# TensorE multiplies the identity with itself in its waits, in a four-stage layer kernel

## The reference

```
m = mean(group); s = var(group)          # over all 128*128 points and the 2 channels
norm(v) = (v - m) / sqrt(s + eps)
x = x + L0(norm(x))   # layer norm, then attention along the rows: 4 heads of 32, softmax, gate, output product
x = x + L1(norm(x))   # windowed attention (8 windows, top 4) folded with a 3x3 depthwise convolution
x = x + L2(norm(x))   # per row of 4 x 32: top 9 of a correlation, an ODE of 8 Runge-Kutta steps as a polynomial
x = x + L3(norm(x))   # products of x and its transpose, of row, column and diagonal sums; relu
```

## Time and profile before

| | |
|---|---|
| time, median of 3 runs (lowest to highest) | 1100.49 us (1098.49 to 1101.67) |
| time of the profiled execution | 1099.39 us |
| its span, first to last instruction | 1097.3 us |
| TensorE busy | 1027.7 us, 94% of the span |
| TensorE weight loads | 731.4 us, 67% |
| VectorE | 762.3 us, 69% |
| ScalarE | 510.6 us, 47% |
| GpSimd | 409.7 us, 37% |
| mean granted clock of TensorE | 0.967 |

### The profile page before, as it was taken

How to read it: one execution, slowest core, us unless ns; L and a number is a source line. 1 busy time by engine, 2 the same in 40 slices (tenths; PEclk the granted TensorE clock), 3 DMA queues, 4 the chain that set the end, 5 groups by cost and what they waited for, 6 DMA issues and landing times. The chain is left out here.

```text
span 1097.3 us, 24506 instructions
## 1 busy us (share of the span) xinstructions
PE 1027.7 (94%) x8864; PEld 731.4 (67%) x8864; DVE 762.3 (69%) x3657; ACT 510.6 (47%) x1101; POOL 409.7 (37%) x555
## 2 busy tenths in 40 slices
PE   5897999999999699779999999999999999999978
PEld 3434888888887343356777777777777777677743
DVE  2686999999998423456767676767776676767445
ACT  2475776776776201133433434343443434343346
POOL 0054666766666200011323333232323233332328
PEclk9899999999999699959999999999999999999979
DMA  8000000000000000000000000000000000000025
GB/s 177 2 0 2 3 2 3 2 3 3 2 3 2 1 1 1 10 1 2 1 1 1 1 1 1 1 1 1 1 1 1 1 1 1 1 1 1 1 56 174
DMA packets 14044, 12.99 MB, mean 12 GB/s; under 512 B 3300, under 2 KB 11748, under 8 KB 13924
## 3 DMA queue, kind: packets, MB, share of 16 engines
q1 hardware_dynamic: 12548, 10.84, 4.0%
q10 hardware_dynamic: 1376, 0.59, 0.3%
HBM read 5.14 MB, written 4.19 MB: 9 GB/s over the span
## 5 line engine op out<-in xcount | busy, mean ns | idle before, releaser
L1615 PE MATMUL quad<-theta,nat 128*128 128x512 f32 x512 | 240.8, 593 | 0.0
L738 POOL TENSOR_TENSOR nat<-nat,arena 128x512 f32<-128x512 f32 x128 | 131.4, 1048 | 48.2 <-DVE arena L793 48.2
L1623 PEld LDWEIGHTS quad<-flat 128*128 128x128 f32 x768 | 104.3, 190 | 46.9 <-ACT flat L1409 24.1
L1615 PEld LDWEIGHTS quad<-theta,nat 128*128 128x128 f32 x512 | 87.5, 191 | 61.7 <-issue 61.7
L1623 PE MATMUL quad<-flat 128*128 128x128 f32 x768 | 124.6, 285 | 2.1 <-ACT flat L1409 1.0
L793 DVE CUSTOM_DVE_ANT_0 nat<-quad,arena 128x128 f32<-128x128 f32 x512 | 112.7, 286 | 6.4 <-PE quad L881 6.4
L1409 ACT ACTIVATE flat<-quad 128x256 f32<-128x256 f32 x192 | 73.4, 383 | 74.5 <-PE quad L1623 58.0
L755 ACT ACTIVATE nat<-pair 128x512 f32<-128x512 f32 x128 | 69.5, 596 | 66.5 <-PE pair L889 66.5
L1366 POOL COPY img<-flat 64x256 f32<-64x256 f32 x63 | 25.0, 398 | 186.2 <-DVE nat L1524 171.7
L760 ACT ACTIVATE nat<-nat 128x512 f32<-128x512 f32 x128 | 77.0, 630 | 4.0 <-POOL nat L738 4.0
L1531 DVE MAX8 arena<-nat 128x8 f32<-128x128 f32 x128 | 28.0, 281 | 71.3 <-ACT nat L1445 71.3
(11 more groups left out here) (386 smaller groups left out, 2300.7 us busy)
## 6 DMA issues: line engine op xcount, KB each, us to landing
out<-nat SPq DMA_DIRECT2D x16, 256.0 KB, 2.0
flat<-img SPq DMA_DIRECT2D x2, 640.0 KB, 8.6
flat<-img SPq DMA_DIRECT2D x1, 512.0 KB, 4.9
const<-in_constants ACTq DMA_DIRECT2D x1, 400.5 KB, 3.1
flat<-img SPq DMA_DIRECT2D x1, 256.0 KB, 3.1
arena<-in_L_conv_Ws SPq DMA_DIRECT2D x1, 240.0 KB
nat<-in_x SPq DMA_DIRECT2D x4, 0.2 KB, 12.1
arena<-in_L_conv_Wq ACTq DMA_DIRECT2D x1, 32.0 KB, 6.5
```

The lines of the kernel that those rows point to most:

```text
L738: pool.tensor_tensor(scored, scored, of_head(least[b], h).broadcast_to([128, ROWS, L]), ALU.subtract).then_inc(lowered, 1)
L1615: return pe.matmul(m.quad[:, n, :], vT[:, col(n)], m.theta[:, part, :], start=(part == 0), stop=False, skip_group_check=True)
L1623: last = pe.matmul(m.quad[:, row, place * C:(place + 2) * C], a8[g % 2][:, col(row)], zs[half][k % 2][:, n, :], start=False, stop=(k == 2) ...
```

## The change

A new helper `keep_clock(pe, bank, times)` issues `times` products of the 128 x 128 identity with itself into the first 128 columns of a bank. Nobody reads them, and they carry no semaphore. They are put at these places of TensorE's list:

- at the end of `load_and_prepare`: 6
- in every norm: 2 (layers 0 and 2) or 4 (layers 1 and 3) ahead of the first product's wait, 2 between the two products, 3 behind the second
- in the attention's last step (the one that has no `past` group): 4 ahead of the wait for the copy, 5 ahead of the wait for the output's factor; 6 at the end of the block
- at the end of `layer1`: 13
- in `layer2`, step 0: 6 ahead of `turn_xs(0)`, 13 ahead of the wait for the diagonal, 9 at the end of the step; 11 at the end of the block

Apart from that the two products with the shift column in `layer1` now load this column 128 times (a broadcast operand), and so write all 128 rows of the banks 4 and 5 in place of row 64 alone. The row that is read is the same.

```diff
+    def keep_clock(self, pe, bank, times):
+
+        ident = self.k("ident", 128)
+        for _ in range(times):
+            pe.matmul(bank[:, 0:128], ident, ident, start=True, stop=True)
@@ load_and_prepare, tensor
             turn_banks(at_bank, BANKS)
+            m.keep_clock(pe, m.bank[4], 6)
@@ group_norm, tensor
+            m.keep_clock(pe, m.bank[7], 2 if layer % 2 == 0 else 4)
             pe.wait_ge(S("mean"), layer + 1)
             pe.matmul(acc[0:rows, 0:1], alike, mv[:, 0:1], start=True, stop=True).then_inc(S("group_mean"), 1)
+            m.keep_clock(pe, m.bank[7], 2)
             pe.wait_ge(S("var"), layer + 1)
             pe.matmul(acc[0:rows, 1:2], alike, e, start=True, stop=True).then_inc(S("group_var"), 1)
+            m.keep_clock(pe, m.bank[7], 3)
@@ layer0_attention, tensor, in the loop
                 if older:
+                    if not past:
+                        m.keep_clock(pe, m.bank[7], 4)
                     pe.wait_ge(rwide_ready, g - 1)
...
                 if older:
+                    if not past:
+                        m.keep_clock(pe, m.bank[7], 5)
                     pe.wait_ge(gated_ready, g - 1)
@@ behind the loop
+            m.keep_clock(pe, m.bank[7], 6)
@@ layer1, tensor
-            pe.matmul(B[4][C:C + 1, :], fold[:, 128:129], m.taps1[:, 0:512], start=True, stop=True)
-            pe.matmul(B[5][C:C + 1, 0:C], fold[:, 128:129], m.taps1[:, 512:TAPS * C], start=True, stop=True).then_inc(S("row_made"), 1)
+            fold_row = fold[:, 128:129].broadcast_to([C + 1, 128])
+            pe.matmul(B[4][:, :], fold_row, m.taps1[:, 0:512], start=True, stop=True)
+            pe.matmul(B[5][:, 0:C], fold_row, m.taps1[:, 512:TAPS * C], start=True, stop=True).then_inc(S("row_made"), 1)
@@ behind its loop
                 close(i)
+            m.keep_clock(pe, B[7], 13)
@@ layer2, tensor, in the loop
                 if s == 0:
+                    m.keep_clock(pe, B[1], 6)
                     turn_xs(0)
...
+                if s == 0:
+                    m.keep_clock(pe, B[1], 13)
                 if p is not None:
                     pe.wait_ge(diag_added, p + 1)
...
                     if c == LAST:
                         horner(c, 1, 2)
+                if s == 0:
+                    m.keep_clock(pe, B[1], 9)
+            m.keep_clock(pe, m.quad[:, 0, :], 11)
```

## The result

| | before | changed |
|---|---|---|
| median | 1101.08 us (1098.49 to 1103.51, 4 runs) | 1091.69 us (1091.51 to 1094.11, 4 runs) |
| ratio | | 0.992, 95% interval 0.9895 to 0.9944 |
| profiled execution, span | 1099.39, 1097.3 us | 1094.11, 1092.3 us |
| mean granted clock | 0.967 | 0.972 |

The change, 105 added products in all, makes the kernel faster by 9.4 us, 0.8%. A second measurement of the same source (e11_changed_again) gave 1092.08 us and a ratio of 0.9918 (0.9897 to 0.9939). The forecast was 1089.0.

The account below looks back on a forecast made before the run. TensorE bounds the loops; at the seams engines wait and its clock halves. Layers 0 to 3 gain 2.0 + 2.0 + 3.3 + 3.8 = 11.1, less 0.2 and 0.5: 10.4, from 1099.39 to 1089.0 us; range 1083.5 to 1096.

Parts of the forecast that it names:

- Layer 3: Start of layer 3: TensorE's cold work up to GpSimd's first diagonal runs warm; gain 3.8 us with the norm, no hole.
- the norm: Each of the four norms: two products each 0.2 us faster, 0.4 us per norm, contained in the layers' gains.
- Layer 1: Behind norm 1: 5.7 us if the clock held, but one short fall expected there; gain taken as 2.0 us.
- the rival with all holes closed: The clock holds in layers 1 and 2 as well; gain 15.5 us, 1083.9 us; chance 15%.
- Layer 2: Norm 2 and layer 2's start: 4.7 us if warm, but a probable clock fall around 472 us; gain taken as 3.3 us.
- the overhang of the thirteen: Layer 2, before L1741: after a fall six of the thirteen added products run cold and end late, costing 1.4 us.
- Layer 0: Behind norm 0: 3.52 us of L543 at the lower clock, TensorE-bound, gives 1.6; with the norm 2.0 us.
- Clock 1.00 from 38 to 55: Sign in the trace after: the higher clock held from 38 to 55 us, around norm 0 and layer 0.
- about 11 us earlier: Sign in the trace after: L1863, at layer 3's start, first comes about 11 us earlier than before.
- The shift column: Layer 1, L1221: four weight loads grow from one column to 128; cost 0 to 1 us, taken as 0.2.
- The slower rival: The clock falls before or within the added products, which stand in the way; 11.0 us slower, 1110.4 us; chance 6%.
- Transpositions and the clock: Layer 2's hole: by the skill's rule its share is about 1.3 us smaller, 1090.3 us; by the rows it stays 1089.0.

Follow-up runs that it names:

- e1_small: The changed kernel with every added product multiplying only an 8 x 8 corner of the identity; 1098.89 us, ratio 0.9995.
- e3_layer3_alone: The kernel before plus only the eleven products behind layer 2's loop and norm 3's four, two and three; 1095.87 us, ratio 0.9965.
- e6_holes: The changed kernel with three more products behind norm 1's barrier and those of layer 2's step 0 spread anew; 1089.28 us, ratio 0.9888.
- e2: The changed kernel with the shift column loaded once again, all added products kept; 1091.68 us, ratio 0.992.
- e5: The changed kernel with 25 more products in waits at the layer norm's end and the attention's first two steps; 1088.99 us, ratio 0.9884.
- e7: e5 and e6_holes joined, eight products instead of six ending the load stage, one set of layer 1 side products moved; 1086.46 us, ratio 0.9861.
- e9: e7 plus 24 warm-up products of ones before the image arrives and identity products in the power chain's waits; 1087.90 us, ratio 0.9894.
- e8_doubled: The changed kernel with twice as many added products at every place; 1102.15 us, ratio 1.0017.

## Why the prediction was right, point by point

- **The mechanism** stood: the time lay in work at the lower clock behind each norm, and filling the waits with array work moves it (e1_small, e3_layer3_alone).
- **Layer 3**: forecast 3.8, measured 3.8 in every one of the ten profiles with those products at their changed number (8.15 to 8.17 us to GpSimd's first diagonal, before 11.97). The number was reached by another sum: 3.6 from the stretch between the first mixed product and the diagonal (8.75 to 5.17; forecast 4.0, to be cut to 3.5 by ScalarE's copies) and 0.2 from the norm (forecast 0.4). That the two came out alike is luck.
- **Layer 1**: forecast 2.0 with one fall, measured 2.5; the fall came, for 6.8 us. With products in the hole it is 5.1 (e6_holes), where the rival with all holes closed put 5.7.
- **Layer 2**: forecast 3.3, measured 2.2. The fall came at 471.8, where it was forecast, and the overhang of the thirteen was 1.3 (forecast 1.4). The 1.4 was lucky in part: ten of them ran cold, not six, but an added product costs 0.43 us cold and 0.23 warm in a row, not 0.52 and 0.29. Mis-sized was the rest: without overhang norm 2 to `theta` is 24.9 us (e2, e5, e6, e7, e9), against 28.3 before: a gain of 3.4 and not of 4.7. Of the 3.4, 1.3 lie ahead of L1761's transpositions (L1741 before; forecast 1.6), where GpSimd ends the wait, and 2.1 behind them (forecast 3.05).
- **Layer 0**: forecast 2.0. Norm 0 to var is 5.66 us where the clock held, in six of the nine profiles of the changed kernel and its extensions, and 8.4 to 8.6 in the other three, where it fell all the same; without the products it is 7.0 to 8.1. So a gain of 1.9 in two of three executions and a small loss in the third. "Clock 1.00 from 38 to 55" was wrong for the profiled execution. The likely hole is the barrier at the end of the load stage: in the three profiles with a fall TensorE stood idle there for 0.95, 1.14 and 1.61 us, in the six others for 0.30 to 0.80. No run changed this idle time alone.
- **The sum**: 2.5 + 2.2 + 3.8 and about 1 for layer 0 make 9.5; measured 9.4. The forecast of 10.4 was high by layer 0's third execution and by layer 2, and low by 0.5 in layer 1. The 1089.0 is off by 2.7 us: 1.0 is the gain, 1.7 is that I took the gain off one execution of 1099.39, while the median of the kernel before came out at 1101.08. GpSimd's first diagonal was to come "about 11 us earlier"; in the profile it came 5.0 earlier, for layer 0's falls are in it.
- **What I didn't see**: the attention's start. The profile of before happened to have a clock of 1.00 there, and I took it as given. It falls in some executions, with the added products of norm 0 and without them (e3_layer3_alone), and costs 4 to 5 us when it does.
- **The shift column**: taken as 0.2 us of cost, it is nothing (e2_nocolumn). **The slower rival** is real when products are added beyond the wait (e8_doubled) or run cold on a busy engine (e9_load), and in small even in the changed kernel, in the 1.3 us of the thirteen.
- **Transpositions and the clock**: the prediction set the rule of the Trainium skill, "TensorE: Matmul & The Clock Gate", Part 4, that transpositions don't count as activity for the clock as products do, against the rows. The traces keep speaking against it: in the kernel before TensorE did nothing but transpositions from 32.4 us until the clock rose at 37.8, in the changed kernel from 31.2 until it rose at 34.9. Layer 2's gain of 2.2 lies near the 2.0 that the rule would have given, but for the reason above, a sum of 3.4 in place of 4.7. None of the runs removed transpositions, so how much they count stays open.

## What to carry to other kernels

In this kernel work behind a synchronisation point pays twice: for the wait, and for the products that then run at half the clock; the second part can be had back with products nobody reads, if they do real array work and end inside the wait. Size each group by the idle time printed before the waiting instruction and the warm duration of one product in a row (here 0.23 us), spread them so that no place is left bare, and put none where TensorE has no idle time. Judge it stage by stage between fixed marks of several profiles, since whether the clock falls at a weak place differs from execution to execution.

## What the hardware showed that I had not expected

- The page's clock before the first clock record of a trace reads 1.00. In the kernel before, the first record is at 37.8 us, and the transpositions ahead of it ran at the lower clock (1.75 us for eight). The true mean clock is lower than the 0.967 printed.
- The low stretches measured 3.4 to 27.3 us. The clock also fell on a busy TensorE: in the kernel before at 406.4, behind 3.7 us of back-to-back products with one moving column each, with TensorE busy in 2.00 of 2 us there:

```profile
402.42 1.94 PE L1260 MATMUL quad<-const,arena 1*128 1x1 f32 x16
404.23 1.92 PE L1263 MATMUL quad<-const,arena 1*128 1x1 f32 x16
```

- Stages that are saturated repeat to 0.1 us over the profiles (568.2 to 568.3 us from the first `theta` to norm 3 in all but e8_doubled, 570.7, whose extra products don't fit in the wait at the end). The differences between executions lie outside them: in the load stage, at the seams, at the attention's start and near 404 us.
